# GpSimd takes the low parts of q and the least scales, ScalarE the bf16 codes, and VectorE adds the bias one batch sooner

## The reference, cut to what matters

```python
bias = braak_embed[braak_stages][..., None]          # one row of embed per batch, S values
q = query + bias                                     # query = x
attn = softmax(einsum('bsd,btd->bst', q, key))       # key = value = fside
h = einsum('bst,btd->bsd', attn, value) @ H          # H: Hadamard 256 x 256
scale = clip(max(abs(h), axis=-1), 1e-05) / 7
xq = clip(round(h / scale), -8, 7) * scale
out = x + einsum('bsi,oi->bso', xq, ternary(weight))
```

## Time and profile before

| | us |
|---|---|
| median of 3 executions | 115.98 |
| lowest, highest | 114.5, 118.74 |
| the profiled execution | 115.06 |
| its span | 113.2 |
| TensorE busy in the span | 93.7 (83%) |
| VectorE busy | 97.3 (86%) |
| ScalarE busy | 66.9 (59%) |
| GpSimd busy | 69.8 (62%) |

### The profile page before, as it was taken

One profiled execution on the slowest core, in us unless ns is written; L12 is line 12 of the kernel. 1 busy time (PEld: TensorE's weight loads), 2 busy tenths in 40 slices (PEclk: granted clock), 3 DMA queues, 4 the chain that ended last, 5 costly groups with the idle time before them and its releaser, 6 DMA issues.

```text
span 113.2 us, 2363 instructions
## 1 busy us (share of the span) xinstructions
PE 93.7 (83%) x681; PEld 81.8 (72%) x681; DVE 97.3 (86%) x230; ACT 66.9 (59%) x171; POOL 69.8 (62%) x92
## 2 busy tenths in 40 slices
PE   5699989962999988699797979799797979798850
PEld 2279978951989877698686868788696868697620
DVE  2695499699699899989999999989999999999872
ACT  3545839743665656584856656565748475567730
POOL 4452247996384938577484839395776848435580
PEclk9999999999999999999999999999999999999999
DMA  3984242047937669575829296746558524455225
GB/s 85 268 286 132 91 106 80 6 151 219 265 112 219 198 206 132 215 197 175 242 97 318 94 276 141 217 149 211 164 186 231 188 46 157 80 179 192 93 93 185
DMA packets 16919, 18.91 MB, mean 167 GB/s; under 512 B 8196, under 2 KB 8848, under 8 KB 16912
## 3 DMA queue, kind: packets, MB, share of 16 engines
q1 hardware_dynamic: 16576, 18.55, 55.8%
q10 hardware_dynamic: 336, 0.28, 0.8%
HBM read 12.92 MB, written 4.19 MB: 151 GB/s over the span
## 4 chain that ended last, share of the span: by engine, by line
DVE 38%; POOL 16%; issue 16%; PE 10%; ACT 9%; DMA 5%; POOLq 1%; ACTq 1%; DVEq 0%
DVE least_scale L872 7%; POOL f_lo L333 7%; DVE prob_lo L845 7%; DVE neg_max L877 6%; ACT prob L669 5%; DVE scaled L831 4%; DMA code_t<-code 3%; PE score_bank L485 3%; DVE abs_max L804 3%; ACT fh_hi L663 3%; POOL result L370 2%; DMA embed_sb<-embed_dram 2%; POOL code L362 2%; DVE raw_scale L824 2%; POOL out_scale L340 2%
## 5 line engine op out<-in xcount | busy, mean ns | idle before, releaser
L370 POOL TENSOR_TENSOR result<-scaled,x_all 128x512 f32<-128x512 f32 x13 | 20.0, 1537 | 20.7 <-DVE scaled L831 20.4
L669 ACT ACTIVATE prob<-score_bank,neg_max 128x256 f32<-128x256 f32 x30 | 14.0, 470 | 20.0 <-DVE neg_max L877 20.0
L333 POOL TENSOR_TENSOR f_lo<-ft,f_hi 128x512 fp32r<-128x512 f32 x15 | 19.1, 1274 | 4.3 <-ACT f_hi L638 4.3
L647 ACT ACTIVATE code<-xh_bank,inv_scale 128x256 f32<-128x256 f32 x30 | 12.6, 472 | 11.4 <-DVE inv_scale L828 11.3
L474 PE MATMUL prob_bank<-ident,prob 128*128 128x128 f32 x64 | 10.3, 284 | 8.8 <-ACT prob L669 7.1
L362 POOL TENSOR_TENSOR code<-code,magic 128x512 bf16<-128x512 f32 x13 | 13.5, 1040 | 4.5 <-ACT code L647 4.5
L845 DVE TENSOR_TENSOR fh_lo<-fh_bank,fh_hi 128x512 fp32r<-128x512 f32 x16 | 11.0, 691 | 5.7 <-ACT fh_hi L663 5.6
L474 PEld LDWEIGHTS prob_bank<-ident,prob 128*128 128x128 f32 x64 | 6.8, 141 | 11.4 <-ACT prob L669 9.3
L485 PE MATMUL fh_bank<-had,f_hi 128*128 128x256 f32 x64 | 14.9, 315 | 0.0
L485 PE MATMUL score_bank<-f_hi,q_hi 128*128 128x256 f32 x60 | 13.7, 310 | 0.0
L485 PE MATMUL fh_bank<-had,f_lo 128*128 128x256 f32 x64 | 13.3, 290 | 0.0
(11 more groups left out here) (119 smaller groups left out, 225.4 us busy)
## 6 DMA issues: line engine op xcount, KB each, us to landing
ft<-f_turned_dram SPq DMA_DIRECT2D x16, 256.0 KB, 2.6
xt<-x_turned_dram SPq DMA_DIRECT2D x16, 256.0 KB, 3.0
x_all<-x_dram SPq DMA_DIRECT2D x16, 256.0 KB, 3.6
out_dram<-result SPq DMA_DIRECT2D x14, 256.0 KB, 2.0
w_t<-weight_turned_dram SPq DMA_DIRECT2D x1, 256.0 KB, 4.8
out_dram<-result SPq DMA_DIRECT2D x2, 128.0 KB, 1.8
out_dram<-last_result ACTq DMA_DIRECT2D x2, 128.0 KB, 1.8
code_t<-code SPq DMA_TRANSPOSE x13, 3.5
```

The costliest lines, as they stand in the source:

```text
L333: nc.gpsimd.tensor_tensor(f_lo[:, b.k], ft[:, b.k], f_hi[:, b.k].bitcast(F32), ALU.subtract).then_inc(f_lo_ready, 1)
L370: nc.gpsimd.tensor_tensor(result[:, b.k], as_rows(scaled[:, b.k]), x_all[:, b.at], ALU.add).then_inc(result_ready, 1)
L647: return nc.scalar.activation(to[:, t], xh[:, t], ACT.Copy, bias=MAGIC, scale=inv_scale[:, b.k, t:t + 1])
L669: a = nc.scalar.activation(prob[:, t], score_bank[:, t], ACT.Exp, bias=neg_max[:, b.k, t:t + 1], accum_out=row_sum[:, b.k, t:t + 1])
```

## The change

VectorE loses two operations per batch: `split_q` and the `least_scale` half of `sums`; both go to GpSimd, the second as a product with a constant tile. GpSimd loses the bf16 codes, which ScalarE now makes with a second activation, `plain_codes`. `add_bias` and the high part of q work on batch i+1 instead of i. The orders of the stages change on three engines, and the opening is rewritten: the score of batch 0 stands ahead of its Hadamard product, the embed parts are made with one subtraction on a 38-row layout, and `xt` is loaded ahead of the Hadamard block.

```diff
 ScalarE
+            def plain_codes(b):
+                wait(act, code_ready, b.at + 1)
+                wait(act, code_turned[b.k], 16 * b.half)
+                nc.scalar.activation(as_rows(code16[:, b.k]), as_rows(code), ACT.Copy, bias=-MAGIC
+                                     ).then_inc(code16_ready, 1)
...
             STAGES_IN_ORDER = (
-                (split_prob, LAG_MIX), (quantize, LAG_QUANT), (split_q, LAG_PARTS),
-                (exponentials, LAG_SCORE), (split_fh, LAG_SCORE), (split_f, LAG_NEXT))
+                (split_prob, LAG_MIX), (quantize, LAG_QUANT), (split_f, LAG_NEXT),
+                (plain_codes, LAG_QUANT), (exponentials, LAG_SCORE), (split_fh, LAG_SCORE),
+                (split_q, LAG_NEXT))
...
             split_f(b1)
+            split_q(b1)
+            exponentials(b0)
             split_fh(b0)
-            split_q(b1)
-            act.wait_ge(weight_loaded, 16)
-            nc.scalar.activation(w_abs[:, :, :], w_t[:, :, :], ACT.Abs).then_inc(w_abs_ready, 1)
-            exponentials(b0)
             split_f(b2)
             split_fh(b1)
             split_q(b2)
+            act.wait_ge(weight_loaded, 16)
+            nc.scalar.activation(w_abs[:, :, :], w_t[:, :, :], ACT.Abs).then_inc(w_abs_ready, 1)
             split_prob(b0)
             exponentials(b1)
             split_f(b3)
+            split_q(b3)
             step(peeled(3))
 VectorE, opening
-            nc.vector.tensor_scalar(embed_low[:, :], embed_sb[:, :], is_low[:, 0:1], None, ALU.mult
-                                    ).then_inc(embed_low_ready, 1)
...
-            nc.vector.scalar_tensor_tensor(
-                out=embed_parts[:, :], in0=embed_hi[:, :].bitcast(F32), scalar=sign[:, 0:1],
-                in1=embed_low[:, :], op0=ALU.mult, op1=ALU.add).then_inc(embed_ready, 1)
+            nc.vector.tensor_tensor(embed_parts[LOW_ROW:ROWS], embed_sb[LOW_ROW:ROWS],
+                                    embed_parts[LOW_ROW:ROWS].bitcast(F32), ALU.subtract
+                                    ).then_inc(embed_ready, 1)
 VectorE
             STAGES_IN_ORDER = (
-                (scales, LAG_QUANT), (add_bias, LAG_PARTS), (split_prob, LAG_MIX), (sums, LAG_MIX),
-                (maximum, LAG_SCORE), (scale_out, LAG_OUT), (split_q, LAG_PARTS),
+                (scales, LAG_QUANT), (split_prob, LAG_MIX), (inverse_sums, LAG_MIX),
+                (maximum, LAG_SCORE), (scale_out, LAG_OUT), (add_bias, LAG_NEXT),
                 (split_fh, LAG_SCORE))
...
             add_bias(b1)
+            maximum(b0)
             split_fh(b0)
-            split_q(b1)
-            maximum(b0)
             add_bias(b2)
             split_fh(b1)
-            split_q(b2)
+            maximum(b1)
             split_prob(b0)
-            sums(b0)
-            maximum(b1)
+            inverse_sums(b0)
+            add_bias(b3)
             weight_rows()
             step(peeled(3))
 GpSimd
+            def split_q(b):
+                wait(pool, q_hi_ready, b.at + 1)
+                nc.gpsimd.tensor_tensor(q_lo[:, b.k], q[:, b.k], q_hi[:, b.k].bitcast(F32),
+                                        ALU.subtract).then_inc(q_lo_ready, 1)
+
+            def least_scales(b):
+                wait(pool, prob_ready, b.at + 1)
+                wait(pool, raw_scale_ready, b.at - 1)
+                nc.gpsimd.tensor_tensor(least_scale[:, b.k], row_sum[:, b.k], least[:, :], ALU.mult
+                                        ).then_inc(least_ready, 1)
...
             def step(batch, dma_turns=True):
+                if b := batch(LAG_MIX):
+                    least_scales(b)
                 if b := batch(LAG_LOAD):
                     pick_rows(b)
                 if b := batch(LAG_PARTS):
-                    split_f(b)
+                    split_q(b)
                 if b := batch(LAG_QUANT):
                     if dma_turns:
                         out_scales(b)
-                if (b := batch(LAG_QUANT)) and dma_turns:
-                    wait(pool, code_ready, b.at + 1)
-                    wait(pool, code_turned[b.k], 16 * b.half)
-                    nc.gpsimd.tensor_tensor(
-                        as_rows(code16[:, b.k]), as_rows(code), magic[:, :].broadcast_to([P, W]),
-                        ALU.subtract).then_inc(code16_ready, 1)
+                if b := batch(LAG_PARTS):
+                    split_f(b)
...
+            split_q(Batch(0, 1))
             split_f(Batch(0, 1))
+            split_q(Batch(0, 2))
             split_f(Batch(0, 2))
+            least_scales(Batch(0, 0))
             pick_rows(Batch(0, 4))
             weight_signs()
 TensorE, opening
+            pe.wait_ge(first_f_lo_ready, 1)
+            pe.wait_ge(first_q_lo_ready, 1)
+            score(b0)
             pe.wait_ge(had_ready, 3)
-            pe.wait_ge(first_f_lo_ready, 1)
             times_hadamard(b0)
-            score(b0)
             biases(b2)
             times_hadamard(b1)
+            score(b1)
             weight_sums()
             turn_prob(b0)
-            score(b1)
             biases(b3)
             mix(b0)
             step(peeled(3))
```

More of the change, by code:

```diff
@@ L47, in adaln_ffn_kernel @@
     B, S, D = x.shape
-    STAGES = embed.shape[1]
+    ROWS = embed.shape[0]
     O = weight_turned.shape[2]
@@ L399, in _ @@
                 step(peeled(i), dma_turns=i - LAG_QUANT < turned_by_dma)
[L400 to L408 removed]
+            fourth_last, third_last, second_last, last = (Batch(0, B - n) for n in (4, 3, 2, 1))
+            least_scales(second_last)
+            least_scales(last)
+            out = fourth_last
+            wait(pool, scaled_ready, out.at + 1)
+            wait(pool, x_loaded[out.k], 16 * out.half + 16)
+            wait(pool, stored[out.k], 16 * out.half)
+            nc.gpsimd.tensor_tensor(result[:, out.k], as_rows(scaled[:, out.k]), x_all[:, out.at],
+                                    ALU.add).then_inc(result_ready, 1)
             pool.wait_ge(last_raw_ready, T)
@@ L930, in _ @@
                 step(peeled(i))
-            with dve.Fori(LOOP_FROM, B // 2) as half:
+            with dve.Fori(LOOP_FROM, B // 2 - 1) as half:
                 for odd in range(2):
                     step(looped(half, odd))
+            for i in range(B - 2, B):
+                step(peeled(i))
             fourth_last, third_last, second_last, last = (Batch(0, B - n) for n in (4, 3, 2, 1))
@@ L1015 @@
     tiles, chunks = rows // P, width // P
+    stages = L0_cond_braak_embed.shape[0]
+    embed = L0_cond_braak_embed.reshape(stages, P, tiles).transpose(0, 2, 1)
     arrays = {
@@ L1020 @@
         "itok": itok_B_0_5,
-        "embed": np.stack([L0_cond_braak_embed.reshape(-1, P, tiles).transpose(0, 2, 1)] * 2),
+        "embed": np.concatenate([embed, np.zeros((LOW_ROW - stages,) + embed.shape[1:], embed.dtype), embed]),
         "weight_turned": L0_ffn_weight.reshape(-1, chunks, P).transpose(2, 1, 0),
```

81 lines of the change are left out of this document (27 added, 54 removed).

## The result

| | before | after |
|---|---|---|
| median (lowest to highest), us | 115.5 (114.5 to 118.74), 4 runs | 127.49 (127.17 to 128.23), 4 runs |
| ratio after to before | | 1.108, 95% interval 1.097 to 1.119 |
| profiled execution (span), us | 115.06 (113.2) | 127.77 (125.9) |

The kernel became slower by 12.0 us, twice the 6.15 that was forecast. The direction and the two loops were right; several terms were too small.

What follows compares the result with a forecast made beforehand. VectorE's queue was taken as the bound. Opening delays and 6.3 us steps put the tail at 104.9, 6.55 late; less 0.4 in the tail, 6.15 on 115.06 gave 121.2 us, range 114.5 to 125.

Steps and rivals of the forecast that it cites:

- The wait that moved: ScalarE, each step: high part of f waits for the Hadamard product, 1.6 after the ternary product begins, holding codes and exponentials.
- the exponentials' loop: Step start to ternary, Hadamard product, high part of f, bf16 codes, exponentials, hand-over to the next step: 6.03 us.
- the signs that the prediction named: High part of f idles, exponentials no longer wait for VectorE, `out_bank` waits for transpose, VectorE idles, step 7 near 49.
- The transpose loop: Ternary product through Hadamard product, high part of f, codes and transpose (3.5): 6.34 us; 6.3 per step taken, against 6.16.
- Opening up to step 3: Start of the kernel: step 3 would begin at 20.35 instead of 17.74, 2.6 us late.
- Step 3 to step 4: Opening: step 4 would begin at 27.95 instead of 23.79; the chain over GpSimd's weight signs ends at 27.7.
- Step 4 to step 5: Opening: first transpose issued at 29.0 behind three loads, takes 3.7, reaches TensorE at 32.7; step 5 begins at 36.45.
- rival 4: TensorE's clock falls back in the opening's longer idle times, costing 2.3: 123.5 us; chance 0.05.
- Steps 5 to 7: Step 5 at 36.45, step 6 at 42.75, step 7 at 49.05 instead of 42.88: 6.2 us late.
- step 15: Last step before the tail: begins at 99.45, takes TensorE's own 5.43, so the tail begins at 104.9.
- Tail: End of the kernel: ScalarE 0.6 ahead of TensorE instead of just behind; 0.4 us credited.
- Rival 1: Steady steps: the wait costs nothing and TensorE sets the step, 5.43; 111.9 us, faster; chance 0.08.

Runs made afterwards that it cites:

- Experiment 3: Changed kernel with each step's code transpose issued ahead of that step's loads on SyncE's queue: 121.55 us.
- experiment 2: Changed kernel with the high part of f moved last in ScalarE's step, behind codes, exponentials and high part of fh: 119.12 us.
- experiment 1: Changed kernel with the bf16 codes put ahead of the high part of f in ScalarE's order: 123.97 us.
- experiment 6: Changed kernel with the earlier opening orders on TensorE, ScalarE and VectorE, plus the earlier first loads (stage ids before embed rows, Hadamard block before xt): 122.93 us.
- experiment 7: Changed kernel with high part of f last, transposes ahead of loads, and the opening orders and first loads of before: 103.07 us.
- experiment 10: Changed kernel with only the first loads put back (stage ids before embed rows, Hadamard block before xt): 127.15 us.
- experiment 12: Kernel of experiment 7 with the low parts of f of batches 1 and 2 ahead of the low parts of q on GpSimd: 103.0 us.
- experiment 4: Changed kernel with the opening's orders of before put back on TensorE, ScalarE and VectorE: 122.1 us.
- experiment 9: Changed kernel with products of zeros filling TensorE's idle time before the ternary weights and the first ternary product: 124.73 us.
- experiment 5: Changed kernel with high part of f last on ScalarE and transposes ahead of the loads on SyncE: 108.16 us.
- experiment 8: Control: the kernel before the change, with transposes ahead of the loads on SyncE's queue: 113.92 us.
- experiment 11: Changed kernel with high part of f last, transposes ahead of loads and the earlier opening orders, but not the earlier first loads: 103.3 us.

## Why the prediction was wrong in size

By its own steps, against the profiled execution of after (127.77, 6.57 over the 121.2):

- **The wait that moved: right.** The high part of f idles for the Hadamard product (18.1 us in all), the exponentials no longer wait for VectorE in the steady part, and VectorE has idle time. Experiment 3 measured the exponentials' loop alone at 6.13 (6.03 forecast), experiment 2 took it away. Of the signs that the prediction named only one failed: step 7 began at 54.08, not near 49.
- **The transpose loop: right, a little short.** 6.3 a step was taken "a shade under 6.34"; 6.46 was measured from step 7 to 15, 1.24 in eight steps. The term that failed is the landing, taken as one median, 3.5, for all steps. In steps 8, 11 and 13 the transpose took 2.8 or 2.9 and the step 6.13 or 6.14, held by the exponentials' loop; in steps 9, 10, 12 and 14 it took 3.4 to 3.9 and the step 6.37 to 6.88. (Step 7's took 3.0, but was issued late, behind a load of x that stood 2.09 in the queue.) So early landings earned nothing back, and late ones lengthened the step. In after the landing went with the loads: six transposes issued 0.5 to 0.9 us after the load of x took 3.4 to 5.2, four issued 1.1 to 2.2 after it took 2.8 to 3.0, and a sooner transpose only waited longer behind the loads, as experiment 1 showed (median 3.9).
- **Opening up to step 3: 2.48 short** (20.35 forecast, 22.83). This is the largest miss, and it stands at the start of the chain. "The wider layout has the same columns and costs nothing" failed, and that the stage ids now come second on their queue was put at nothing without a word. By the forecast q of batch 0 would have begun at 5.46 (5.98 in before, less the 0.52); it began at 7.45, behind the row picks, which started at 5.60 when the stage ids had come. In eight executions with this order it began between 6.66 and 7.45, 7.1 in the middle; in the four with the ids first (experiments 6, 7, 10 and 12) between 6.48 and 6.72. So some 1.1 of the 2.0 is the embed rows, which in these four were converted at 4.70 to 5.08, against 3.81 before; some 0.5 is the ids' order, and the rest scatter. The score of batch 0 began at 9.32, where 7.2 was forecast, and its maximum at 12.26, where 9.9 was, 2.36 late; the chain behind that was read right to 0.1. Step 3 itself came between 22.11 and 24.13 in seven runs with this opening, so a microsecond of it either way is scatter.
- **Step 3 to step 4: right.** 7.6 forecast, 7.69 measured; the chain over GpSimd's weight signs was read well.
- **Step 4 to step 5: 1.9 short**, by two terms. The first transpose was priced at 3.7, the one row of before, where three loads also stood just ahead of it; it took 5.2. Against that it was issued 0.3 sooner after the step's start than forecast. Behind three loads it took 3.3 to 5.5 in eight kernels (the two of the change and experiments 1, 2, 4, 6, 9 and 10), so one row was too few to price it; what sets it within that range is not shown. And rival 4, the clock, was given 0.05 because an idle of 2.37 in before had not brought it down. Here it fell after an idle of 2.79 (granted 0.73 from 31 to 36 us), and was down again after one of 2.18 (0.66 from 36 to 41 us). Experiment 9 prices it at 0.67 in that step, and not at the 2.3 of the rival's sum, as the slow products ahead of the ternary product ended within the wait for the transpose. The Trainium skill ("TensorE: Matmul & The Clock Gate", "HAM oscillation — how this bites in real kernels") says that long waits between bursts put the array back to half rate; after's trace agrees (pairs of products at 0.63 in place of 0.40). One row that shows no fall was poor evidence all the same: experiment 10 shows none behind the same idle of 2.79, only one after the wait that followed.
- **Steps 5 to 7: 0.6 short, step 15: 0.6 short.** The landing again: the transpose that step 6 waited for took 4.1 (from 46.03), and in step 15 the ternary product waited 1.15 for one that took 4.1 (from 104.79). Before that last one no load had been issued for 4.8 us, and in the same place it took 4.1 to 4.6 in experiments 3, 4, 6 and 10 and 2.4 in 1, 2 and 9; what holds it is not shown. The 5.43 used for TensorE's own step was too long as well: it runs to the end of the last pair of products, which in back-to-back steps overlaps the next turn, and experiments 5 and 7 show 5.10 from turn to turn.
- **Tail: right.** 14.13 from its first turn to the end, 14.85 before; 0.4 was credited.

The terms add up: 2.48 + 0.09 + 1.89 + 0.57 + 1.24 + 0.62 - 0.32 = 6.57. Rival 1 (TensorE sets the step) is what the change can do once both queues are reordered; as it stood, its condition, a Hadamard product done before the float32 codes, did not hold.

What stays open: what sets the landing of the first transpose and of step 15's, why the first 0.7 us came sooner in experiment 9, and what sets how long TensorE's products stay at 0.63 in the first 20 us (to 13 us in after, to 20 in experiment 10). None of these was tried.

## What to carry to other kernels

When work leaves the bound engine, look at each queue that receives it for a wait that stands ahead of the new work: an operation that waits for this step's product belongs last in an in-order queue, and a transfer that the next step needs belongs ahead of loads that have a batch of slack. Two loops of nearly equal length hide each other, so undo parts in pairs as well as singly: here 8.4 and 5.9 alone made 19.3 together, which turned a loss of 11% into a gain of 5%, and the opening's orders made it 10%. Price an opening by the landing times of its own queue order and check what each idle gap does to TensorE's clock, for errors there are paid once but in full.

## What the runs showed of the hardware

- The bf16 transpose of one batch's codes took 2.5 to 2.9 (median) from issue to landing where it stood ahead of the loads, in six kernels (experiments 3, 5, 7, 8, 11, 12). Behind loads the median was 3.2 to 3.9 (after, experiments 1, 2, 4, 6, 9, 10), and the first one, with three loads issued just before it, took 3.3 to 5.5.
- The granted clock fell in step 4 behind an idle of 2.79 on TensorE in after, and behind idles of 1.2 to 1.4 and 0.6 in experiments 5 and 12. It did not fall there behind the same 2.79 in experiment 10, behind the 2.55 of experiment 4, or behind 1.3 and 0.6 in experiments 7 and 11. So the length of one idle does not tell it. With the gaps filled by products it stayed at 1.00 in the profiled execution (experiment 9).
- At the start of the execution pairs of products took 0.63 while the granted-clock column read 1.00 (experiment 10, to 20 us); in experiments 3, 4 and 11 the column read 0.50 there, from 8 to 10 us. So at the start only the durations of the rows tell the pace.
